# Another merged order for the steps of two batches in a two-layer decoder

## The chip, the cores and the metric

The kernel runs on one core of a Trainium2 chip. The metric is the device time of one launch in microseconds (us): the median of three launches. A profiled launch gives the trace from which all rows below are read; its span goes from the first to the last instruction. The engines are TensorE (PE, matrix products), VectorE (DVE), ScalarE (ACT, functions from tables), GpSimd (POOL) and SyncE (SP, which only issues DMA transfers).

## The reference

Six blocks follow each other on an input of 2 batches × 512 tokens × 128 features, each as `x = layernorm(x + f(x))`:

```
x = _layernorm(x + _L0_attn_ref(x, ...))    # Hawk: rmsnorm, conv of 4, gates, linear recurrence, gated MLP
x = _layernorm(x + _L0_xattn_ref(x, ...))   # cross attention, 8 heads, 32 context rows
x = _layernorm(x + _L0_ffn_ref(x, ...))     # causal attention, 16 heads of 8, RoPE; then 7 experts, top 2, + shared
x = _layernorm(x + _L1_attn_ref(x, ...))    # selective SSM, 16 states:
...
        h = a_t * h + bx_t
        y = jnp.einsum('bdn,bn->bd', h, c_t)
...
x = _layernorm(x + _L1_xattn_ref(x, ...))   # masked cross attention, FiLM, S4D convolution, FFN
x = _layernorm(x + _L1_ffn_ref(x, ...))     # 8 experts, top 2, and 2 shared ones:
...
        eo = jnp.einsum('eti,eih->eth', jax.nn.silu(hg) * hu, wd)
        y = jnp.einsum('te,eth->th', wdense, eo)
        shared = jax.nn.silu(xf @ swg) * (xf @ swu) @ swd
```

## The kernel before, in words

x stays on the chip transposed: features on the 128 partitions, 512 tokens along the free dimension (often in two halves of 256). There are three lanes of work. Lane a is batch 0 and lane b is batch 1; each goes through the six blocks. Lane w holds what depends on weights alone: the masks and constants of the gates, the tables of the S4D convolution (cosines, sines, powers, differences and their spectra), and the context tables.

Each compute engine's program is written as three generators, one for each lane. Every `next` of a generator issues one step (mostly one to eight instructions) and its waits; a step ends with an increment of a semaphore that belongs to its engine and lane. There are 541 steps on PE, 575 on DVE, 465 on ACT and 97 on POOL. The table `TURNS` gives for each engine the order in which the three lanes take their turns: `"a8 w1 a5"` is eight steps of batch 0, one shared step, five steps of batch 0. Inside a lane the order is fixed. `TURNS` is the only thing that decides which instruction stands behind which on an engine, and as an engine runs its instructions in order, a step that waits holds back all that is behind it, of the other lanes too. Waits name a step and not a place, so any merged order computes the same. A wait in a step is for a semaphore's count of another engine and lane (`pe.wait_ge(*after("act", b, f"su{n - 2}"))`).

`TABLES` belongs to ACT. Its functions come from four table sets (`exp`, `log`, `gelu`, `sin`); Exp is in `exp` and in `log`. `"232:exp"` loads the set for exp before step 232. A table load is an instruction of its own (L1203).

SP has one list of transfers in a fixed order, each behind the step that it waits for. It is not in `TURNS`.

Names that the text uses, by stage:

- Hawk: `h1` (first rmsnorm: square, log, exponents `ra`, `r`), z and g (projections), x1 (first residual), h2, X1 (the layernormed output). Helper lines are ACT L1207, DVE L1553 (tensor_tensor), L1556, L1559, L1562 (reduce), POOL L2195.
- Self attention: k1, k2, q1, q2 (RoPE products) give kk and qq, of which `kr, qr, kl, ql` take off high and middle parts, so that each is three bf16 pieces. SP writes the pieces to DRAM (L572, `draft_k`, `draft_q`) and reads them back stacked over partitions (L579). For batch 0 DVE does the splitting, for batch 1 POOL. On the stacked operands PE computes `mx` units (L821, L824: scores whose maximum DVE takes, eight pairs of heads × A to E) and then `su` units (L838, L841: 40 scores per batch, of which ACT takes the exponent), `pv` (L852, values), nmt1 (L859, the maxima turned over), yT and yt (transposes), mo (output projection).
- First experts: `sl` and `hu`, `hw` with L924, L929, L956; `rt` is the router; ln3 and X3 the layernorm behind them.
- SSM: dl, dx, `sc0` to `sc15` (DVE scans, L1878), `hc` (products with C), `by` (POOL products); X4 is the output.
- Shared S4D work: `s1..` on ACT, `r`, `q` and `P`, `Q`, `tP`, `tQ`, `aP`, `aQ` (DVE L1556 and L1559 on 1024 columns, POOL L2281); `z`, `a`, `dc` are small tables of 128 × 128.
- Second cross attention `xb`, FFN, and the second experts: 14 units of 128 per batch, with three pairs of 512-column products each (L924, L929, L956).

Every stage of batch 1 runs somewhat behind that of batch 0, and the order of the turns is what interleaves them.

Of the kernel before, what the change touches and what calls it, by code (L numbers as in the profile page):

```python
# [162 lines left out]
def _centre(t):  # L163
# [59 lines left out]

TURNS = {
# [8 lines left out]
    "dve":  # L233
# [8 lines left out]
    "act":  # L242
# [6 lines left out]
    "pool":  # L249
        "w13 b3 w1 b2 w1 b1 w37 a1 w1 a4 w1 a7 w1 a4 b1 a1 w1 b16 w1",  # L250
}

TABLES = (
# [4 lines left out]


def steps_of(engine, lane):
# [2271 lines left out]
```

## Time and profile before

| | |
|---|---|
| time, median of 3 (lowest, highest) | 487.06 us (486.44, 488.05) |
| span of the profiled execution | 484.9 us |
| median less the span | 2.2 us |
| mean granted TensorE clock | 0.927 |
| busy PE | 413.4 us, 85% |
| busy DVE | 333.5 us, 69% |
| busy ACT | 293.4 us, 61% |
| busy POOL | 125.2 us, 26% |
| table loads in the chain: ACT L1203 | 3% of the span |

The profiled execution gives no time besides its span; what lies around the span is taken as the 2.2 us between it and the median. Of the chain of work that ended last, PE has 58%, DVE 19%, ACT 12%. A busy share is a mean over stages with different limits; the stages are told apart by windows of 20 us. In a row of the timeline the first number is the start, the second the duration (of several merged instructions with `xN`), and the brackets at the end hold the idle time before it on its engine and what ended it.

### The profile page before, as it was taken

What the parts mean: (1) busy time and instruction counts of PE and PEld (TensorE: products, weight loads), DVE (VectorE), ACT (ScalarE), POOL (GpSimd) and SP (SyncE); (2) the same over time, 40 slices, a digit from 0 to 9 for tenths busy, and PEclk for the clock granted to TensorE, in tenths of its full rate; (3) what the DMA queues carried; (4) which work ended last, traced back from release to release, by engine and by line L of the source; (5) the groups of instructions that cost most, each with busy time, mean ns of one, the idle gap of its engine ahead of it and who ended that gap; (6) DMA issues with size and microseconds to landing.
All of it is one profiled execution on the core that took longest, in us unless ns stands there. A gap on an engine that the chain in (4) does not pass through costs nothing.

```text
span 484.9 us, 5925 instructions
## 1 busy us (share of the span) xinstructions
PE 413.4 (85%) x2035; PEld 202.0 (42%) x2035; DVE 333.5 (69%) x616; ACT 293.4 (61%) x508; POOL 125.2 (26%) x129
## 2 busy tenths in 40 slices
PE   5968988888889999999977875557889899999995
PEld 2443533443345554434343221232666544544442
DVE  1386567789969953562799999899977543564454
ACT  4865697526245678889576896456347575652125
POOL 1100000000382029007966667745000200000000
PEclk9999999958789999999997996667989999999999
DMA  8950000564181000005008857979500000501401
GB/s 280 341 153 30 1 2 0 170 90 150 50 191 25 2 4 3 2 15 161 0 18 239 211 168 214 213 206 278 230 0 1 1 0 17 159 1 53 123 0 43
DMA packets 26109, 46.62 MB, mean 96 GB/s; under 512 B 7397, under 2 KB 12742, under 8 KB 24918
## 3 DMA queue, kind: packets, MB, share of 16 engines
q1 hardware_dynamic: 25972, 46.15, 33.6%
q8 instruction: 16, 0.26, 0.3%
q10 hardware_dynamic: 108, 0.10, 0.1%
q14 instruction: 13, 0.11, 0.1%
HBM read 41.13 MB, written 5.01 MB: 95 GB/s over the span
## 4 chain that ended last, share of the span: by engine, by line
PE 58%; DVE 19%; ACT 12%; issue 5%; POOL 3%; DMA 2%; SPq 1%; DVEq 0%; ACTq 0%
ACT AR L1207 7%; DVE AR L1553 7%; PE PS L924 7%; PE PS L956 6%; PE PS L929 5%; PE PS L852 4%; PE PS L838 4%; PE PS L821 3%; ACT L1203 3%; PE PS L688 3%; PE PS L1007 2%; DVE stats L1562 2%; DVE AR L1559 2%; POOL AR L2195 2%; DVE AR L1878 2%
## 5 line engine op out<-in xcount | busy, mean ns | idle before, releaser
L1207 ACT ACTIVATE AR<-PS 128x512 f32<-128x512 f32 (+3 forms) x187 | 98.9, 563 | 103.3 <-PE PS L924 49.5
L1553 DVE TENSOR_TENSOR AR<-PS,AR 128x512 f32<-128x512 f32 (+1 forms) x104 | 69.1, 675 | 49.6 <-PE PS L929 30.4
L2195 POOL TENSOR_TENSOR AR<-AR 128x512 f32<-128x512 f32 (+2 forms) x48 | 52.5, 1101 | 137.3 <-DVE AR L1553 106.7
L1207 ACT ACTIVATE AR<-AR 128x256 f32<-128x256 f32 (+3 forms) x110 | 46.7, 463 | 44.3 <-DVE AR L1553 28.0
L1203 ACT ACT_TABLE_LOAD x42 | 53.9, 1283 | 0.8
L1562 DVE TENSOR_REDUCE stats<-PS 128x1 f32<-128x512 f32 (+4 forms) x88 | 43.6, 521 | 10.3 <-PE PS L762 4.3
L1878 DVE TENSOR_TENSOR_SCAN AR<-PS,AR 128x512 f32<-128x512 f32 x32 | 38.8, 1212 | 1.3 <-ACT PS L1207 0.7
L821 PE MATMUL PS<-RR 97*128 97x512 bf16 (+3 forms) x128 | 34.1, 344 | 4.2 <-DVE stats L1562 3.3
L688 PE MATMUL PS<-AR,W_sq 128*128 128x256 f32 x88 | 27.3, 424 | 10.8 <-ACT AR L1207 6.3
L1553 DVE TENSOR_TENSOR AR<-AR 128x512 f32<-128x512 f32 (+2 forms) x48 | 32.3, 689 | 3.9 <-ACT AR L1207 2.6
L1207 ACT ACTIVATE AR<-PS,W_vec 128x256 f32<-128x256 f32 (+1 forms) x46 | 24.2, 545 | 12.6 <-PE PS L688 4.3
L838 PE MATMUL PS<-RR 100*128 100x512 bf16 (+3 forms) x128 | 29.5, 302 | 2.5 <-ACT AR L1207 2.3
L2281 POOL TENSOR_TENSOR RR<-KL,lags 128x512 f32<-128x512 f32 x24 | 29.4, 1262 | 1.2 <-PE PS L841 1.1
L929 PE MATMUL PS<-x_in,RR 128*128 128x512 f32 x56 | 28.6, 596 | 0.0
L956 PE MATMUL PS<-AR,RR 128*128 128x512 f32 x56 | 28.5, 596 | 0.0
L1207 ACT ACTIVATE PS<-AR,RA 128x512 f32<-128x512 f32 x32 | 21.5, 684 | 11.5 <-DVE AR L1878 7.7
L924 PE MATMUL PS<-x_in,RR 128*128 128x512 f32 x56 | 28.4, 595 | 0.0
L688 PEld LDWEIGHTS PS<-AR,W_sq 128*128 128x128 f32 x88 | 15.9, 201 | 24.9 <-ACT AR L1207 16.2
L824 PE MATMUL PS<-W_bf 128*128 128x256 bf16 (+1 forms) x80 | 22.5, 282 | 0.0
L852 PE MATMUL PS<-AR,Vaug 128*9 128x512 f32 (+3 forms) x256 | 21.8, 434 | 0.0
L841 PE MATMUL PS<-W_bf 128*128 128x256 bf16 (+1 forms) x80 | 20.2, 252 | 0.0
L1710 DVE TENSOR_REDUCE stats<-PS 128x1 f32<-128x384 f32 x32 | 17.5, 548 | 3.5 <-PE PS L824 3.3
(241 smaller groups left out, 712.8 us busy)
## 6 DMA issues: line engine op xcount, KB each, us to landing
AR<-scan SPq DMA_DIRECT2D x64, 256.0 KB, 3.9
RR<-in_ffn SPq DMA_DIRECT2D x1, 2688.0 KB, 11.1
RR<-in_ones SPq DMA_DIRECT2D x2, 832.0 KB
RR<-in_ones SPq DMA_DIRECT2D x2, 784.0 KB
RA<-in_moe SPq DMA_DIRECT2D x1, 1539.5 KB, 6.2
AR<-weights SPq DMA_DIRECT2D x6, 256.0 KB, 4.8
W_mla<-in_mla SPq DMA_DIRECT2D x1, 1504.0 KB, 15.9
W_late<-in_late SPq DMA_DIRECT2D x1, 1076.0 KB, 11.5
```

The costliest lines, as they stand in the source:

```text
L688: mm(own(b, i)[:, c], w("sq", "ones"), A(b, 1)[:, c], start=True, stop=True)\
L821: mm(ring[:, c:c + n_], Qst[b][0:MROWS, h, 128 * qt:128 * qt + 128], Kst[b][0:MROWS, h, 0:n_], start=(qt, c) == segs[0][1:], stop=False)
L838: mm(ring[:, c:c + n_], Kst[b][0:KROWS, h, 128 * kb:128 * kb + 128], Qst[b][0:KROWS, h, 128 * kb:T], start=(c == 0), stop=False)
L924: mm(own(b, 0), w(group, "g", 128 * k, 128), x, start=True, stop=True)\
L929: mm(own(b, 1), w(group, "u", 128 * k, 128), x, start=True, stop=True)\
L956: mm(own(b, 3), w(group, "d", 128 * j, 128), A(b, 6 + j % 2), start=(j == 0 and base is None), stop=(k == n))\
L1203: nc.scalar.preload_act_table_set(tables[loaded[0]])
L1207: nc.scalar.activation(out_, in_, func, bias=bias, scale=scale).then_inc(*done("act", *step))
L1553: nc.vector.tensor_tensor(out_, a, b_, op).then_inc(*done("dve", *step))
L1562: nc.vector.tensor_reduce(out_, a, X, op).then_inc(*done("dve", *step))
L1878: nc.vector.tensor_tensor_scan(A(b, 14 + i % 2), own(b, 1 + 2 * (i % 2)), scan_row(b, "dx", i), 0.0, ALU.mult, ALU.add).then_inc(*done("dv ...
L2195: nc.gpsimd.tensor_tensor(out_, a, b_, op).then_inc(*done("pool", *step))
```

## The change

Only `TURNS` (all four engines) and `TABLES` are different. Steps, their waits, tiles, buffers and SP's list of transfers are as they were. Since the tables got shorter by three lines, every line of the file after it has a number smaller by three.

```
 TURNS = {
     "pe":
-        "a8 w1 a5 w2 a2 w1 a3 w1 a4 w2 a2 b2 a1 b2 a2 b1 a2 b1 a2 b2 a2 b2 ...
+        "a9 w1 a4 w3 a6 w1 a3 w2 a2 b2 a2 b2 a3 b2 a2 b1 a2 b3 a2 b1 a1 b1 ...
...
 TABLES = (
-    "2:log 11:gelu 12:log 14:gelu 17:exp 26:log 40:gelu 47:log 51:gelu 52:exp 64:log 91:gelu 100:log "
-    "125:sin 133:log 230:sin 232:exp 239:sin 245:exp 247:sin 254:log 272:sin 280:exp 282:sin 283:exp "
...
+    "2:log 11:gelu 14:exp 26:log 40:gelu 47:log 51:gelu 53:exp 65:log 92:gelu 96:sin 101:log 105:sin 107:log "
+    "230:sin 233:exp 240:sin 245:exp 248:sin 252:log 255:sin 257:log 273:sin 280:exp 282:sin 283:exp 285:sin "
...
```

The list has 42 table switches before and 45 after.

ACT, the first microseconds of the program (AR0 and x_in0 are batch 0, AR1 and x_in1 batch 1, `small` holds shared constants, `AR0<-AR0 128x256` are the exponents ra and r of h1). Before:

```order
2 L1207 ACTIVATE AR0<-x_in0 128x256 x2
3 L1203 ACT_TABLE_LOAD
4 L1207 ACTIVATE AR0<-PS 128x256 x2
5 L1207 ACTIVATE AR1<-x_in1 128x256
6 L1207 ACTIVATE AR0<-AR0 128x256 x2
7 L1207 ACTIVATE small<-W_vec 128x2
8 L1207 ACTIVATE AR0<-PS,W_vec 128x512 x2
9 L1207 ACTIVATE small<-small 128x2
10 L1203 ACT_TABLE_LOAD
11 L1207 ACTIVATE AR0<-PS 128x512
12 L1203 ACT_TABLE_LOAD
```

After:

```order
4 L1204 ACTIVATE AR0<-PS 128x256
5 L1204 ACTIVATE small<-W_vec 128x2
6 L1204 ACTIVATE AR0<-PS 128x256
7 L1204 ACTIVATE small<-small 128x2
8 L1204 ACTIVATE AR0<-AR0 128x256
9 L1204 ACTIVATE small<-small,W_vec 128x2
10 L1204 ACTIVATE AR0<-AR0 128x256
11 L1204 ACTIVATE AR0<-PS,W_vec 128x512 x2
12 L1200 ACT_TABLE_LOAD
13 L1204 ACTIVATE AR0<-PS 128x512 x2
14 L1204 ACTIVATE AR1<-x_in1 128x256
```

The square of batch 1's input moved from before the exponents of batch 0 to behind the first gelu of batch 0; three tiny shared exponents moved in between, and one pair of table switches is gone.

DVE around the splitting of batch 0 (`AR0<-AR0 128x512` are kk, qq, kr, qr, kl, ql in this order; `x_in1<-PS,AR1` is X1 of batch 1; `AR1<-AR1 128x128` are shared tables). Before:

```order
79 L1553 TENSOR_TENSOR AR0<-AR0 128x512 x2
80 L1553 TENSOR_TENSOR AR1<-PS,AR1 128x512
81 L1553 TENSOR_TENSOR AR0<-AR0 128x512
82 L1553 TENSOR_TENSOR AR1<-PS,AR1 128x512
83 L1553 TENSOR_TENSOR AR1<-AR1 128x128
84 L1553 TENSOR_TENSOR AR0<-AR0 128x512
85 L1553 TENSOR_TENSOR AR1<-AR1 128x128 x2
86 L1553 TENSOR_TENSOR AR0<-AR0 128x512 x2
87 L1553 TENSOR_TENSOR x_in1<-PS,AR1 128x256 x2
88 L1562 TENSOR_REDUCE stats<-PS 128x16
```

After:

```order
80 L1550 TENSOR_TENSOR AR0<-AR0 128x512 x2
81 L1550 TENSOR_TENSOR AR1<-PS,AR1 128x512 x2
82 L1550 TENSOR_TENSOR AR0<-AR0 128x512 x2
83 L1550 TENSOR_TENSOR x_in1<-PS,AR1 128x256 x2
84 L1550 TENSOR_TENSOR AR0<-AR0 128x512 x2
85 L1559 TENSOR_REDUCE stats<-PS 128x16
```

kl and ql of batch 0 stood ahead of batch 1's X1 and now stand behind it. The small shared tables are gone from here.

PE where the maxima of batch 0 end (L821/L824 with 512, 384+128, 256 columns are the mx units, L838/L841 the su units, L859 is nmt1, L852 pv0.0). Before:

```order
175 L824 MATMUL PS<-W_bf 128x2x128
176 L838 MATMUL PS<-RR 128x512
177 L841 MATMUL PS<-W_bf 128x128
178 L838 MATMUL PS<-RR 128x512
179 L841 MATMUL PS<-W_bf 128x128
180 L838 MATMUL PS<-RR 128x512
181 L841 MATMUL PS<-W_bf 128x128
182 L838 MATMUL PS<-RR 128x512
183 L841 MATMUL PS<-W_bf 128x128
184 L859 MATMUL PS<-W_bf,parts 24x128 x4
```

After:

```order
171 L821 MATMUL PS<-W_bf 128x2x128
172 L835 MATMUL PS<-RR 128x512
173 L838 MATMUL PS<-W_bf 128x128
174 L835 MATMUL PS<-RR 128x512
175 L838 MATMUL PS<-W_bf 128x128
176 L818 MATMUL PS<-RR 128x512
177 L821 MATMUL PS<-W_bf 128x128
178 L835 MATMUL PS<-RR 128x512
179 L838 MATMUL PS<-W_bf 128x128
180 L818 MATMUL PS<-RR 128x384
181 L818 MATMUL PS<-RR 128x128
182 L821 MATMUL PS<-W_bf 128x256
```

Row 176 of after is the first maxima unit of batch 1. Before, it stood behind su5, nmt1 and pv0.0 of batch 0; now it stands behind su1, and the units of the two batches alternate from there.

Other moves that the text speaks of: on ACT, b.rt went from behind a.ln3's exponents to before its logs; on DVE, batch 0's X4 went from behind b.sc3 to behind b.hc4; on POOL, the shared dc1 to dc12 went from behind b.kr to before b.kk, and aP1 and aQ1 went from before a.dx to behind a.by1 and a.by5.

## Rows read from the trace of the kernel before

**Rows 1.** Windows of 20 us, PE: length, busy (instructions), granted clock, DMA share, GB/s.
```profile
180.00:200.00 20.00, 19.74 (x176) 1.00 0.01 3
...
440.00:460.00 20.00, 20.00 (x52) 1.00 0.39 107
```
**Rows 2.** The same windows, DVE.
```profile
100.00:120.00 20.00, 18.60 (x42) 0.76 0.44 118
320.00:340.00 20.00, 19.76 (x25) 0.78 0.89 231
```
**Rows 3.** Timeline, ACT, the exponents of h1 of batch 0.
```profile
8.68 0.42 ACT L1207 ACTIVATE AR<-x_in 128x256 f32<-128x256 f32 x1 [1.76 <-DMA x_in<-in_x]
9.00 0.70 ACT L1207 ACTIVATE AR<-AR 128x256 f32<-128x256 f32 x2
```
**Rows 4.** Timeline, PE, first projection of batch 0.
```profile
9.76 0.82 PE L696 MATMUL PS<-W_sq 128*128 128x512 bf16 x3 [0.70 <-ACT AR L1207]
11.33 1.10 PE L716 MATMUL PS<-AR,RA 128*128 128x512 f32 x2 [0.75 <-DVE AR L1559]
```
**Rows 5.** Timeline, DVE, x1 of batch 0.
```profile
40.34 0.69 DVE L1553 TENSOR_TENSOR AR<-PS,x_in 128x512 f32<-128x512 f32 x1 [1.26 <-PE PS L735]
```
**Rows 6.** Timeline, DVE, RoPE and splitting of batch 0, X1 of batch 1.
```profile
84.66 1.29 DVE L1553 TENSOR_TENSOR AR<-PS,W_mla 128x512 f32<-128x512 f32 x2 [0.93 <-PE PS L792]
...
90.39 2.61 DVE L1553 TENSOR_TENSOR AR<-AR 128x128 f32<-128x128 f32 x6
94.97 0.76 DVE L1553 TENSOR_TENSOR x_in<-PS,AR 128x256 f32<-128x256 f32 x2 [1.97 <-ACT AR L1207]
```
**Rows 7.** Timeline, PE and DVE, the first maxima unit of batch 0.
```profile
100.10 0.61 PE L821 MATMUL PS<-RR 97*128 97x512 bf16 x1 [0.53 <-ACT Vaug L1207]
...
103.43 0.63 DVE L1562 TENSOR_REDUCE stats<-PS 128x1 f32<-128x512 f32 x1
```
**Rows 8.** Timeline, POOL and SP: dc1 after kr of batch 1; last stack transfer of its first heads.
```profile
132.22 0.46 POOL L2195 TENSOR_TENSOR KL<-AR,KL 128x128 f32<-128x128 f32 x1 [1.43 <-ACT AR L1207]
...
138.34 0.42 SPq L579 DMA_DIRECT2D RR<-draft_q  x1
```
**Rows 9.** DMA of 136 to 139 us: issues, KB each, us to landing.
```profile
RR<-draft_k SPq DMA_DIRECT2D x1, 192.0 KB, 4.0
```
**Rows 10.** Timeline, PE, between the maxima of the two batches.
```profile
140.92 0.39 PE L838 MATMUL PS<-RR 100*128 100x512 bf16 x1 [0.41 <-ACT AR L1207]
...
142.68 0.39 PE L859 MATMUL PS<-W_bf,parts 128*24 128x128 bf16 x4 [0.82 <-DVE parts L1553]
...
144.75 0.39 PE L821 MATMUL PS<-RR 97*128 97x512 bf16 x1
```
**Rows 11.** Timeline, PE, the longest wait in the overlap of the two attentions.
```profile
201.75 0.39 PE L838 MATMUL PS<-RR 100*128 100x256 bf16 x2 [0.89 <-ACT AR L1207]
```
**Rows 12.** Timeline, POOL, shared products beside batch 0's third layernorm.
```profile
233.20 15.86 POOL L2281 TENSOR_TENSOR RR<-KL,lags 128x512 f32<-128x512 f32 x12
```
**Rows 13.** Timeline, ACT, the router of batch 1.
```profile
245.82 0.23 ACT L1207 ACTIVATE stats<-stats 128x28 f32<-128x28 f32 x1 [0.48 <-DVE stats L1553]
```
**Rows 14.** Timeline, DVE, up to the first scan.
```profile
243.62 2.07 DVE L1559 SCALAR_TENSOR_TENSOR RR<-RR 128x1024 f32<-128x1024 f32 x1
...
249.20 1.21 DVE L1559 SCALAR_TENSOR_TENSOR RR<-RR 128x1024 f32<-128x1024 f32 x1
...
252.47 0.68 DVE L1553 TENSOR_TENSOR AR<-AR 128x512 f32<-128x512 f32 x1
...
262.33 1.21 DVE L1878 TENSOR_TENSOR_SCAN AR<-PS,AR 128x512 f32<-128x512 f32 x1
```
**Rows 15.** Timeline, ACT, a table switch in the scans.
```profile
280.11 1.28 ACT L1203 ACT_TABLE_LOAD   x1
281.40 0.60 ACT L1207 ACTIVATE AR<-PS 128x512 f32<-128x512 f32 x1
```
**Rows 16.** Timeline, DVE, X4 of batch 0 among the scans of batch 1.
```profile
315.24 0.76 DVE L1553 TENSOR_TENSOR x_in<-PS,AR 128x256 f32<-128x256 f32 x2 [1.72 <-ACT AR L1207]
```

More of the change, by code:

```diff
@@ L225 @@
     "pe":
[7 rows of a table removed]
-    "dve":
[8 rows of a table removed]
-    "act":
[6 rows of a table removed]
[6 rows of a table added]
+    "dve":
[7 rows of a table added]
+    "act":
[5 rows of a table added]
     "pool":
-        "w13 b3 w1 b2 w1 b1 w37 a1 w1 a4 w1 a7 w1 a4 b1 a1 w1 b16 w1",
+        "w25 b4 w1 b1 w2 b1 w22 a3 w1 a4 w1 a1 w1 a2 w1 a2 w1 a4 b1 a1 w1 b16 w1",
 }
 TABLES = (
[4 rows of a table removed]
[4 rows of a table added]
 def steps_of(engine, lane):
```

43 rows, old and new, of tables (TABLES, TURNS) are left out of this document.

## The prediction
> **What bounds the kernel now.** I read the windows of 20 us first. Between about 143 and 206 us PE has no gaps to speak of (19.74 of 20 us busy in one window of it [rows 1]), and in the second experts, from about 400 us, it is busy all the time (20.00 of 20 at 440 to 460 us [rows 1]). In both the same multiplications must be done whatever the order, so there an order can win or lose only what PE waits. In between DVE is the bound: it has 18.60 of 20 us at 100 to 120 us, where it takes batch 0's maxima, and 19.76 at 320 to 340 us in the scans [rows 2]. What is left is chains in which no engine is full: the first 100 us, the first experts of batch 0 (206 to 262 us), the second cross attention (345 to 400 us) and the end behind the last product. Then I read the timelines of the stretches in which the two orders differ, and followed each lane's chain through them. A change of order moves no work off the chip, so its effect is the sum of the waits that it takes from these chains and puts into them. All times of the trace are of the profiled execution, with a span of 484.9 us; the median of the runs is 2.2 us above it, and I add that at the end.
>
> **Step 1, the start: −2.6 us.** ACT waits 1.76 us for batch 1's input and squares it (0.42 us), and only then gives batch 0's exponents at 9.00 us [rows 3]. PE waits for them 0.70 us at 9.76 us, and for DVE's product 0.75 us at 11.33 us [rows 4]. After, three exponents of two columns stand there and the square is behind the first gelu. The exponents can start when ACT is done at 6.92 us (8.68 less 1.76), so up to 2.1 us earlier; the filler products of PE (0.82 us in that row, and those ahead) still stand before the projection, so I take 1.7 us for it. One pair of table switches goes from the same chain (2 × 1.28 us [rows 15]), of which I count 0.9, since ACT waits for PE in that stretch anyway. x1 of batch 0, at 40.34 us before [rows 5], comes 2.6 us earlier. Bounds: −1.0 (only what PE waits after the exponents) and −4.7 (2.1 and both switches).
>
> **Step 2, up to batch 0's maxima: +0 to the sum, but all late things are later.** The small shared tables that DVE did one by one beside kr to ql (six steps in 2.61 us at 90.39, four of them tables [rows 6]) now go earlier, into DVE's waits. In exchange k1 of batch 0 stands before batch 1's input product, so that this waits for what k1 waits for (0.93 us before 84.66 [rows 6]), and batch 1's X1 stands ahead of kl and ql. It waits 1.97 us for ACT at 94.97 [rows 6] and comes over 1 us later for the reason just given. So kl and ql, which ended at 93.00 us (90.39 + 2.61), end at about 98.2, measured in the time of before (that is, with step 1 left out; so are all times up to step 7). The write to DRAM and the stacking behind them move by 5.2 us. PE had its first maxima product at 100.10 us [rows 7], and DVE took it only at 103.43 us [rows 7], since it was still in batch 1's cross attention; this slack of 3.3 us is the cover. The first stack lands at about 103.7 by my count, 3.6 us after 100.10, so the cover is used up and the start of the maxima is about 1 us late. DVE gets that back: it is rid of the small tables that stood between the maxima. The last maximum of batch 0 comes at +0.3 us. Bounds 0 and +2.
>
> **Step 3, the middle: +1.9 us.** This is the step that I believe most. Batch 1's pieces are split on POOL. dc1 waited 1.43 us there at 132.22 us behind kr [rows 8]; dc1 to dc12 now stand before kk, and kk itself comes 1.3 us later, because batch 1 has become later in step 2. I get ql at +1.7 us, and so the last transfer for the first heads at 140.0 instead of 138.34 us [rows 8]. A neighbour of 192 KB took 4.0 us from issue to landing [rows 9]; with 3.6 the stack is there at 143.6 us. On PE batch 1's first maxima unit was at 144.75 us [rows 10], behind su2 to su5, nmt1 and pv0.0 of batch 0, so that it never waited. Now it stands behind su1 alone. PE reaches it at about 140.9 us, where su2 stood [rows 10], waits until 143.6, and has the other units still to do: they take 144.75 − 140.92 − 0.82 (the wait of nmt1) = 3.0 us [rows 10]. So it is at the same point at 146.6 instead of 144.75. From there to 206 us PE is full, and nothing gives it back. Bounds: −0.8 (the stack is there in time, and the wait of 0.82 goes) and +3.3 (the stack lands 1.4 us later than I count, which batch 0's own transfers ahead of it in the queue could do).
>
> **Step 4, the overlap of the attentions: +0.9 us.** The end of batch 0's attention moves ahead by 8 to 16 places among batch 1's score units, and with it ten short steps of ACT squeeze in between its exponents. Before, the longest such wait of PE was 0.89 us at 201.75 [rows 11], and the sum over 180 to 200 us 0.26 us (20 less 19.74 [rows 1]), 1.2 us in all. For after I count 2.1 us. That batch 0 ends sooner brings nothing, since its first sl on ACT stands behind b.su33 in both. Bounds 0 and +1.6.
>
> **Step 5, first experts of batch 0 up to the scans: −0.1 us.** Batch 1's router exponent, which waited for DVE at 245.82 us [rows 13], now stands before the logs of batch 0's ln3. This and POOL's products at the same time make X3 late by some 2.9 us. But X3 was not what DVE waited for: the SSM's dl ran at 252.47 [rows 14] behind a chain of small router operations, and then the shared q at 261 us ran until the scan at 262.33 [rows 14]. POOL's 12 products of 15.86 us [rows 12] lie over this stretch and stretch DVE's operation from 1.21 to 2.07 us (249.20 and 243.62 [rows 14]). Of these twelve, aP1 and aQ1 now go behind by1 and by5, and dl gets +0.9 but the rest −1.0. Bounds −1 and +2.9 (X3's delay in full). On this stretch the Trainium skill ("SBUF — State Buffer", the shared port pair) has a rule that an operation of VectorE with two inputs in SBUF and one of GpSimd fully block each other; the 0.86 us by which the one row is longer than the other agrees in sign, and by the rule aP1 and aQ1 would only move the price into the scans' stretch, where DVE's products with one input in PSUM don't pay it.
>
> **Step 6, the scans: −0.4 us.** DVE is full here, so only its idle time counts. Two more table switches on ACT and a shared sine moved forward cost +0.6 at the tenth scan, and batch 1's products of POOL begin behind the shared Q1: +0.8 at its first scan. Batch 0's X4 waited 1.72 us for ACT at 315.24 [rows 16]; it stands two scans' places later now, with work of batch 1 ahead of it, and this wait goes, of which 0.5 comes back at the next one. −1.2. Bounds −1.7 and +2.5 (a scan waits for both of the switches). A table switch shows here as 1.28 us and the next function starts 0.01 us after it [rows 15]. The Trainium skill ("ScalarE: Activation LUTs", *What ACT_TABLE_LOAD costs*) gives 1283 ns for the load and some 1380 ns for a drain, 2.66 us in all, by which three more switches would take 8.0 us of ACT and not 3.9; the row shows no such drain.
>
> **Step 7, 345 us to the end: +0.1 us.** PE's order is the same in nearly all of this. Units 10 to 13 of batch 0 are drawn ahead and batch 1's come alone at the end; with 20.00 of 20 us busy [rows 1] that is the same sum of products. Bounds 0 and +0.6.
>
> **Sum.** −2.6 + 0 + 1.9 + 0.9 − 0.1 − 0.4 + 0.1 = −0.2 us. The span would be 484.7 us, the time 486.9 us. The change is many small gains and losses of opposite sign, and the early gain is eaten before 145 us. What a measurement tells from no change here is 0.3%, 1.5 us.
>
> **Rivals.** *A, the early gain survives: about 484.2 us.* If the stack lands at about 142 us, since the queue is shorter than I think, step 3 is at 0, and with half of step 4 the sum is −2.6 + 0 + 0.5 − 0.1 − 0.4 + 0.1 = −2.5, and 484.6; with the whole 1.72 us of rows 16 gained 484.2. For it: PE waited 0.82 us for nmt1 in that very place [rows 10], and the new order offers it work there; the landing in step 3 rests on a chain of four delays that I worked out. Against it: kl and ql behind X1, which the order shows plainly.
> *B, PE's queue stalls behind late stacks: about 490 us.* One mechanism, at two places: the operands of the maxima. If kl and ql end 1 us later than 98.2, batch 0's maxima start that much later and DVE, at 18.60 of 20 us [rows 2], has nothing to catch up with; the same at batch 1's unit gives +3.3 in place of +1.9, and a further 1.3 us where the other heads' transfers come later than the exponents of batch 0. −2.6 + 1 + 3.3 + 1.3 + 0.9 − 0.1 − 0.4 + 0.1 = +3.5, and 490.6. It decides from the point where the first stack lands after 104.7. For it: SP's list is in fixed order, so one late piece delays all behind it. Against: the slack of 3.3 us at 103.43.
> *C, batch 0's chain after its attention is what matters: about 489 us.* X3 is late by 2.9 us and DVE is not covered by the router, so the scans start 2 us later: +1.9.
>
> **Chances.** My forecast and what lies within 0.3% of before: 0.37. A, and other ways to over 1.5 us faster: 0.34. B 0.18, C 0.08, others slower 0.03, so slower in all 0.29. The case A is so near in chance because the only sure gain is at the start and all that eats it is counted. The range goes from 483.8 (A) to 490.2 (nearly B); the forecast's own range is 485.6 to 488.5.
>
> **What would show it.** Step 1: x1 of batch 0 near 37.7 us. Step 2: kl, ql of batch 0 end near 95.6 on the new clock (98.2 − 2.6), and the first maximum of DVE near 101.9. Step 3: a wait of PE of about 2.5 us before batch 1's first maxima unit, and that unit near 141 us. Step 4: waits of some 2 us in all from 176 to 206 us. Step 5: first scan near 262.4. Step 6: no wait for ACT at X4, last scan of batch 1 within 0.5 us of before. The forecast is wrong if PE doesn't wait at batch 1's first unit, or if the first scan is over 1.5 us away from 262.3.

## The result, and the profile after

The changed kernel took 494.38 us (median of 4 runs, 491.55 to 500.76) against 487.56 us for the kernel before (4 runs, 486.44 to 488.23). The ratio is 1.0126, with a 95% interval from 1.0089 to 1.0163: 6 to 7 us slower. A second set gave 495.22 us (6 runs, 492.60 to 500.47) against 486.79 us, ratio 1.017 (1.012 to 1.022). I had forecast 486.9 us, no change. Medians are over all runs of a kernel; the ratios leave out runs that are over 1.5% above its fastest one.

The first profiled execution of the changed kernel was the slowest of its runs (span 498.9 us). The rows below are from its second trace (span 494.3 us, mean granted clock 0.927, the same as before), where not said otherwise. The first trace is late from the start (+1.6 us at x1, +4.8 at batch 0's last maxima unit) and ends at +14.1. All line numbers of the changed kernel are smaller by three. The columns are as ahead of the prediction. "Lag" is the time at which a step ends, less the time of the same step in the trace of before.

The start. ACT gives the exponents at 6.89 us and not at 9.00 [rows 3], as forecast; PE's projection begins at 10.23 us (11.33 before [rows 4]); but the projection in front of x1 takes 3.61 us, and x1 of batch 0 is at 40.37 us, where it was before (40.34 [rows 5]). ACT, PE, DVE:

```profile
6.89 0.41 ACT L1204 ACTIVATE AR<-AR 128x256 f32<-128x256 f32 x1
```
```profile
10.23 3.60 PE L713 MATMUL PS<-AR,RA 128*128 128x512 f32 x8
...
36.73 3.61 PE L732 MATMUL PS<-AR,RA 128*128 128x512 f32 x4
```
```profile
40.37 0.69 DVE L1550 TENSOR_TENSOR AR<-PS,x_in 128x512 f32<-128x512 f32 x1 [2.62 <-PE PS L732]
```

The same four products in front of x1 in the trace of before, PE:

```profile
38.05 2.25 PE L735 MATMUL PS<-AR,RA 128*128 128x512 f32 x4
```

Batch 0's kl and ql end at 97.28 us (96.00 + 1.28; 93.00 before [rows 6]) and PE waits 3.95 us for their stack; DVE takes the first maximum at 103.75 us (103.43 before [rows 7]). DVE, then PE, then DVE:

```profile
95.33 0.76 DVE L1550 TENSOR_TENSOR x_in<-PS,AR 128x256 f32<-128x256 f32 x2 [3.76 <-ACT AR L1204]
96.00 1.28 DVE L1550 TENSOR_TENSOR AR<-AR 128x512 bf16<-128x512 f32 x2
```
```profile
102.59 0.58 PE L818 MATMUL PS<-RR 97*128 97x512 bf16 x1 [3.95 <-DMA RR<-draft_q]
```
```profile
103.75 0.68 DVE L1559 TENSOR_REDUCE stats<-PS 128x1 f32<-128x512 f32 x1
```

Batch 1's first maxima unit, which never waited before [rows 10], now waits 2.47 us for its last stack transfer, at 142.40 us. The product of 512 columns takes 0.38 us ahead of the wait, 0.63 us behind it and 0.38 us again later (148.22; the products of 146.14 us are already fast): behind the wait PE ran at half its clock. PE:

```profile
139.50 0.38 PE L835 MATMUL PS<-RR 100*128 100x512 bf16 x1
...
142.40 0.44 PE L818 MATMUL PS<-RR 97*128 97x512 bf16 x1 [2.47 <-DMA RR<-draft_q]
142.74 0.63 PE L835 MATMUL PS<-RR 100*128 100x512 bf16 x1
...
148.22 0.38 PE L818 MATMUL PS<-RR 97*128 97x512 bf16 x1
```

This wait is not in the first trace of after. There PE is at half clock from 130 to 150 us, gets to the unit later and waits 0.65 us, for ACT:

```profile
144.73 0.63 PE L835 MATMUL PS<-RR 100*128 100x512 bf16 x1
...
146.12 0.61 PE L818 MATMUL PS<-RR 97*128 97x512 bf16 x1 [0.65 <-ACT Vaug L1204]
```

The windows of the second trace, PE: granted clock (the number behind the bracket) 0.83 and 0.85, where in before both are 1.00 ([rows 1] for the one from 180 us):

```profile
140.00:150.00 10.00, 7.58 (x49) 0.83 0.83 119
180.00:190.00 10.00, 7.95 (x67) 0.85 0.01 3
```

But the window from 140 us is at 0.83 also in four of the six traces whose order is that of before from 20 to 205 us, and these four have spans of 484.2 to 492.4 us. One of them is the run that only moved a square at the start (485.62 us, below); there PE comes out of a wait of 0.94 us at nmt1 at half clock. PE, window, then timeline:

```profile
140.00:150.00 10.00, 9.15 (x72) 0.83 0.63 93
```
```profile
140.85 0.47 PE L859 MATMUL PS<-W_bf,parts 128*24 128x128 bf16 x4 [0.94 <-DVE parts L1553]
141.25 0.61 PE L838 MATMUL PS<-RR 100*128 100x384 bf16 x2
```

The end of batch 1's maxima: four operations of DVE on 32 columns (nh1, nr1, nm1, nl1) take 1.09, 0.99, 0.96 and 0.98 us, while POOL begins its twelve shared products at 181.42 us, and PE waits for them. DVE, POOL, PE:

```profile
181.43 1.09 DVE L1553 TENSOR_SCALAR parts<-stats 128x32 bf16<-128x32 f32 x1
182.55 0.99 DVE L1556 SCALAR_TENSOR_TENSOR stats<-stats,parts 128x32 f32<-128x32 f32 x1
183.57 0.96 DVE L1565 CAST parts<-stats 128x32 bf16<-128x32 f32 x1
184.56 0.98 DVE L1550 TENSOR_TENSOR parts<-stats,parts 128x32 bf16<-128x32 f32 x1
```
```profile
181.42 13.56 POOL L2278 TENSOR_TENSOR RR<-KL,lags 128x512 f32<-128x512 f32 x12 [27.68 <-PE PS L838]
```
```profile
185.60 0.39 PE L856 MATMUL PS<-W_bf,parts 128*24 128x128 bf16 x4 [1.83 <-DVE parts L1550]
...
187.60 1.11 PE L901 MATMUL PS<-W_sq,AR 128*128 128x128 f32 x4 [0.21 <-DVE AR L1550]
188.64 1.88 PE L849 MATMUL PS<-AR,Vaug 128*9 128x512 f32 x8
```

In the trace of before the first of these four was at 176.70 us and POOL's products began at 180.49 us. DVE, POOL:

```profile
176.70 0.18 DVE L1556 TENSOR_SCALAR parts<-stats 128x32 bf16<-128x32 f32 x1
176.92 0.19 DVE L1559 SCALAR_TENSOR_TENSOR stats<-stats,parts 128x32 f32<-128x32 f32 x1
```
```profile
180.49 13.59 POOL L2281 TENSOR_TENSOR RR<-KL,lags 128x512 f32<-128x512 f32 x12 [1.11 <-PE PS L841]
```

The scans of both batches now wait for POOL, where in before the first of all followed directly upon another operation [rows 14]; X4 still waits 1.22 us for ACT (1.72 before [rows 16]). DVE:

```profile
270.83 1.22 DVE L1875 TENSOR_TENSOR_SCAN AR<-PS,AR 128x512 f32<-128x512 f32 x1 [3.60 <-POOL AR L2192]
...
316.37 1.22 DVE L1875 TENSOR_TENSOR_SCAN AR<-PS,AR 128x512 f32<-128x512 f32 x1 [2.41 <-POOL AR L2192]
...
327.47 0.75 DVE L1550 TENSOR_TENSOR x_in<-PS,AR 128x256 f32<-128x256 f32 x2 [1.22 <-ACT AR L1204]
```

The lag through the trace (us), and that of three mixtures that are explained below:

| step | after | after, block back | before to 205, then after | after to su33, then before |
|---|---|---|---|---|
| x1 of a | 0.0 | −0.7 | −1.0 | −1.0 |
| last maxima unit of a (PE) | −0.6 | −1.5 | −2.1 | −1.9 |
| nmt1 of b | +6.9 | +3.6 | −2.3 | +4.9 |
| su33 of b (ACT) | +7.0 | +2.4 | −2.1 | +5.3 |
| first scan of a | +8.5 | +3.6 | 0.0 | +5.4 |
| first scan of b | +10.3 | +4.8 | +0.5 | +3.9 |
| X6 of b | +9.5 | +5.3 | +0.3 | +5.2 |

### The profile page after: what moved, and what is told of

Its sections match the earlier page's. It is cut to its first block, busy times and chain, and to the rows that moved or that the text cites. A ratio compares the mean times of both kernels' runs of the same rounds, so it can differ in the third digit from the quotient of the medians.

```text
span 498.9 us, 5926 instructions
## 1 busy us (share of the span) xinstructions
PE 422.9 (85%) x2033; PEld 202.5 (41%) x2035; DVE 336.3 (67%) x616; ACT 297.7 (60%) x511; POOL 124.9 (25%) x129
## 4 chain that ended last, share of the span: by engine, by line
PE 62%; DVE 15%; ACT 13%; issue 4%; POOL 4%; DMA 2%; SPq 0%; DVEq 0%; ACTq 0%
ACT AR L1204 8%; PE PS L953 6%; PE PS L921 6%; PE PS L926 6%; DVE AR L1550 5%; PE PS L818 4%; PE PS L835 3%; PE PS L685 3%; PE PS L722 3%; PE PS L849 3%; POOL RR L2278 3%; DVE AR L1875 2%; ACT L1200 2%; PE PS L1004 2%; PE PS L693 2%
## 5 line engine op out<-in xcount | busy, mean ns | idle before, releaser
L1204 ACT ACTIVATE AR<-PS 128x512 f32<-128x512 f32 (+2 forms) x187 | 98.6, 561 | 106.1 <-PE PS L921 44.9
L818 PE MATMUL PS<-RR 97*128 97x512 bf16 (+3 forms) x128 | 35.1, 352 | 7.1 <-DVE stats L1559 3.8
L2278 POOL TENSOR_TENSOR RR<-KL,lags 128x512 f32<-128x512 f32 x24 | 27.7, 1186 | 27.8 <-PE PS L838 27.7
L835 PE MATMUL PS<-RR 100*128 100x512 bf16 (+3 forms) x128 | 30.5, 311 | 2.0 <-ACT AR L1204 1.9
L821 PE MATMUL PS<-W_bf 128*128 128x256 bf16 (+1 forms) x80 | 23.2, 289 | 0.0
L818 PEld LDWEIGHTS PS<-RR 97*128 97x128 bf16 x128 | 11.4, 107 | 25.5 <-DVE stats L1559 14.6
L987 PE MATMUL PS<-AR,RA 128*32 128x512 f32 x64 | 12.6, 871 | 10.3 <-DVE AR L1550 10.3
```

The costliest lines, as they stand in the source:

```text
L818: mm(ring[:, c:c + n_], Qst[b][0:MROWS, h, 128 * qt:128 * qt + 128], Kst[b][0:MROWS, h, 0:n_], start=(qt, c) == segs[0][1:], stop=False)
L835: mm(ring[:, c:c + n_], Kst[b][0:KROWS, h, 128 * kb:128 * kb + 128], Qst[b][0:KROWS, h, 128 * kb:T], start=(c == 0), stop=False)
L1204: nc.scalar.activation(out_, in_, func, bias=bias, scale=scale).then_inc(*done("act", *step))
```

## The experiments

"Mixture" means: the steps up to a place stand in one kernel's order, all others in the other's; steps, waits and buffers are the same in all kernels here, and the table switches follow the order of ACT. Each ratio is to runs of the kernel before on the same chip, with its 95% interval; the runs were made on three chips, so runs of different chips are best compared by their ratios.

**The changed kernel again.** No edit.

> The changed kernel unchanged, to have a second trace of it. Its four runs so far lie between 491.6 and 500.8 us, and the one trace (span 498.9) is the slowest of them. If the loss lies in places (theory P), this trace shows the same waits in a shorter span: PE waits 1.5 to 2 us at batch 1's nmt1, and nh1, nr1, nm1, nl1 take about 1.0 us each on DVE (before 0.19). If the loss is only a lower granted clock of that one run (theory C), this trace has neither and ends within 2 us of before.

495.22 us, ratio 1.017 (1.012 to 1.022). The waits of the first trace are there again in a trace of the same mean clock as before (nmt1 1.83 us, the four small operations about 1.0 us each). For these theory P holds: the loss lies in places. The wait at batch 1's first maxima unit is not one of them: 2.47 us here, 0.65 us in the first trace.

**POOL's products away from the four small operations.**

```
 PE, from batch 1's su0 (a and b are the batches):
-b.su0 a.su38 a.su39 b.su1 b.su2 a.pv3.1 a.pv3.2 b.su3 b.nmt1 a.yT3
+b.su0 a.su38 b.su1 b.su2 b.su3 b.nmt1 a.su39 a.pv3.1 a.pv3.2 a.yT3
```

> The changed kernel, with su39 (and pv3.1, pv3.2 behind it) of batch 0 moved on PE behind nmt1 of batch 1. The last score unit of batch 0 releases POOL's twelve products of the S4D tables. Theory P: these products stretch the four small DVE operations of batch 1's maxima from 0.19 to 1.0 us each, PE waits 1.84 us for them, and its clock falls to half for the 4 us behind: with the move the four are back at 0.2 us, PE does not wait, and the kernel gains 2.5 to 4 us. Theory C or a loss that lies elsewhere: within 0.5 us of the changed kernel.

497.45 us, ratio 1.0169 (1.0114 to 1.0224): no gain in the time. The mechanism is shown all the same: su39 of batch 0 releases POOL, and with it behind, the four take 0.18 to 0.19 us. DVE:

```profile
185.42 0.18 DVE L1555 TENSOR_SCALAR parts<-stats 128x32 bf16<-128x32 f32 x1
185.64 0.19 DVE L1558 SCALAR_TENSOR_TENSOR stats<-stats,parts 128x32 f32<-128x32 f32 x1
185.86 0.18 DVE L1567 CAST parts<-stats 128x32 bf16<-128x32 f32 x1
```

The wait of 1.83 us at nmt1 is gone, and three others come in its place, of PE:

```profile
186.27 0.39 PE L837 MATMUL PS<-RR 100*128 100x512 bf16 x1 [0.53 <-ACT AR L1206]
...
189.61 0.66 PE L867 MATMUL PS<-W_sq,AR 128*128 128x128 f32 x4 [0.72 <-ACT AR L1206]
...
191.79 0.66 PE L903 MATMUL PS<-W_sq,AR 128*128 128x128 f32 x4 [0.86 <-DVE AR L1552]
```

Against the first trace of after, whose start was alike (lag 8.6 and 8.4 us at batch 1's last maxima unit), the lag at su33 is 1.4 us less. I had expected 2.5 to 4.

**Two mixtures around 145 us.**

> All steps that started before 145 us in the trace of before stand in the order of before, the others in the order of after. If the loss is made behind 145 us (theory P: nmt1, then the first experts), this has it nearly whole: 490 to 492 us, 3 to 5 us over before. If it is made ahead of 145 us (theory E: the late pieces of batch 0 and the clock of PE), this is within 1.5 us of before.

495.76 us, ratio 1.0187 (1.0149 to 1.0225). Nearly the whole loss, but not a clean part: its trace has a wait of 3.95 us of DVE for POOL's memset at 148.00 us, which neither kernel has; the seam made it.

> The reverse: all steps that started before 149 us in the trace of after stand in the order of after, the others in the order of before. Theory P: within 1.5 us of before, or a little faster; theory E: 4 us or more slower than before. If both halves cost, each of the two mixtures is slower than before by a part and the parts add up to that of the changed kernel.

491.50 us, ratio 1.0101 (1.0066 to 1.0136). In these six runs the early part costs 4.7 us by itself, against theory P. In its trace the lag is −0.8 us at x1, +2.0 at batch 0's last maxima unit and +3.6 at batch 1's, so over half of it was lost ahead of 142 us (the expectation of the run with the block back, below, says that all was lost between 139 and 159 us; that is wrong). And PE does not wait for the stack at batch 1's first unit. It is at half clock from 128 to 148 us and waits 0.65 us for ACT. PE, timeline, then window:

```profile
143.35 0.61 PE L822 MATMUL PS<-RR 97*128 97x512 bf16 x1 [0.65 <-ACT Vaug L1208]
```
```profile
140.00:150.00 10.00, 9.35 (x48) 0.58 0.84 129
```

**The start alone.**

```
 ACT:
-a.h1.l b.h1.sqa a.h1.ra a.h1.r ... w.fb.l b.h1.sq
+a.h1.l a.h1.ra a.h1.r ... w.fb.l b.h1.sqa b.h1.sq
```

> The kernel before, with one step moved on ACT: the square of batch 1's first half of the input goes from before batch 0's exponents of the first rmsnorm to just before its own second half. My theory of the start (step 1): x1 of batch 0 comes earlier, by 1.2 us (what PE's first projection gained in the traces of after) as long as PE's clock stays high; 1 to 2 us faster in all. Rival (clock): the emptier PE falls to the low clock in the first 40 us (projection rg 3.6 in place of 2.25 us), and the time is within 0.5 us of before or above it.

485.62 us, ratio 1.0018 (0.9984 to 1.0052): no gain. PE's first projection is 2.0 us earlier in this trace, x1 1.1 us; but seven other traces with the old start have x1 at −1.5 to +0.5, so 1 us of start is within what one execution differs from the next. My forecast took it from a single trace.

**Batch 1's first units early, alone.**

```
 PE (with v of batch 1 on ACT ahead of su1):
-a.su0 a.su1 a.su2 a.su3 a.nmt1 a.su4 a.su5 a.pv0.0 b.mx0.A b.mx0.B b.mx0.C
+a.su0 a.su1 b.mx0.A a.su2 b.mx0.B a.su3 b.mx0.C a.nmt1 a.su4 a.su5 a.pv0.0
```

> The kernel before, with the first three maxima units of batch 1 on PE drawn ahead to behind su1, su2 and su3 of batch 0, as in the changed kernel (and v of batch 1 on ACT ahead of su1, which they need). Theory (step 3): PE waits at the first unit for the last stack transfer, issued at 138.34 us; with 3.6 us to land that is until 142 us, a wait of about 1 us, in place of the wait of 0.8 at nmt1 that moves behind it: 0 to +1 us at the same point, since here the stack is not late. Rival (clock): any wait of PE between 140 and 145 us keeps the clock at half for the following 5 us, 2 to 3 us slower.

485.68 us, ratio 1.0018 (0.9983 to 1.0053): no loss. PE waits, but 1.31 us and not 2.47, and the products behind stay at 0.38 us. PE:

```profile
139.41 0.38 PE L822 MATMUL PS<-RR 97*128 97x512 bf16 x1 [1.31 <-DMA RR<-draft_q]
139.69 0.38 PE L839 MATMUL PS<-RR 100*128 100x512 bf16 x1
```

**The block back behind pv0.0, with the early order of after.**

> All steps up to batch 0's last maxima unit on PE (139 us) in the order of after, the others in the order of before, so that batch 1's first unit stands behind pv0.0 again. The mixture that changed over at 149 us was 4.7 us slower than before, and its trace lost all of this between 139 and 159 us. Theory (step 3: the unit's place makes the loss): this one is 2 to 4 us faster than that mixture, 488 to 489.5. Rival (the late stack and the low clock at 130 to 150 us make it, wherever the unit stands): 491 us again.

485.81 us, ratio 0.9985 (0.9944 to 1.0026). Its 12 runs fall into two groups, 481.7 to 485.8 (7) and 489.4 to 493.9 (5). The ratio counts the lower group alone; the mean of all twelve is 487.6 us, against 485.8 for the kernel before.

The mixture at 149 us differs from this one by the place of the block (and of v of batch 1 on ACT). Its median is 5.7 us higher, but that is not shown to be the price of the place. Its six runs (489.9 to 494.0, on another chip) lie where the upper group of this one lies. The two traces, both of runs in that range, need 68.3 us (149) and 67.8 us (this one) from batch 0's last maxima unit to batch 1's su33, only 0.6 us apart, both at half clock for most of 128 to 150 us. This one's window, PE:

```profile
140.00:150.00 10.00, 9.84 (x45) 0.51 0.97 170
```

Whether the early block makes the upper group come more often (6 of 6 runs against 5 of 12) is not settled. That late kl and ql of batch 0 cost nothing by themselves is shown by the two runs at the end of this section.

**The same in the changed kernel, and both mends.** mx0.A to mx0.D of batch 1 behind pv0.0 of batch 0; then also su39 as above.

> The changed kernel, with the first four maxima units of batch 1 on PE put back behind pv0.0 of batch 0, as in the kernel before. The order up to 139 us alone cost nothing (485.8), the order up to 149 us cost 4.7 us, and what lies between the two is this block. Theory (the place of the block, met by a late stack): 3 to 5 us faster than the changed kernel, 490 to 492. Rival (the block alone is harmless, as it was in the kernel before, and the loss comes from the two orders of PE behind 145 us): less than 1.5 us faster.

490.78 us, ratio 1.0084 (1.0053 to 1.0116), against 1.017 (1.012 to 1.022) for the second set of the changed kernel: by these, 4 us of the 8 are this block. Against its first set (1.0126, 1.0089 to 1.0163) it is 2 us, and the intervals overlap. In the traces the stretch from batch 0's last maxima unit to batch 1's su33 takes 71.3 us, against 75.1 and 74.0 in the two traces of the changed kernel.

> The same, and su39, pv3.1 and pv3.2 of batch 0 behind nmt1 of batch 1, so that POOL's twelve products no longer stand beside the four small DVE operations. Theory: 1.2 to 3 us faster than with the first mend alone (that is what the trace of that mend gained), 488 to 490. Rival: the waits only move to the next places, as at su3, yT3 and yt in the trace of the single mend, and the gain is under 0.5 us.

492.54 us, ratio 1.0125 (1.0082 to 1.0169). The second mend gains nothing on top of the first; the rival was right, as the same three waits of 0.53, 0.72 and 0.86 us take the place of one that was only 0.88 us here.

**Behind 205 us.**

> All steps that started before 205.5 us in the trace of before in the order of before, the others in the order of after. In the second trace of after the lag was 7.0 us at the end of batch 1's scores and 9.5 at the end, with 8.5 at the first scan and 10.1 at the last. Theory: the order behind 205 us costs by itself 2 to 3.5 us (POOL's shared products in the scans delay by0 of batch 1, X3 late): 489 to 490.5. Rival (what follows is only the lag carried on, with PE's clock): within 1 us of before.

488.48 us, ratio 1.0087 (1.0051 to 1.0124). The order behind 205 us costs 2 to 4 us by itself. Both waits for POOL are there (its lag rises from −2.1 at su33 to 0.0 at the first scan), DVE:

```profile
262.29 1.22 DVE L1877 TENSOR_TENSOR_SCAN AR<-PS,AR 128x512 f32<-128x512 f32 x1 [3.49 <-POOL AR L2194]
...
306.61 1.22 DVE L1877 TENSOR_TENSOR_SCAN AR<-PS,AR 128x512 f32<-128x512 f32 x1 [2.40 <-POOL AR L2194]
```

> The order of after up to batch 1's su33 (214 us in its trace), then the order of before. The reverse mixture was 2 to 4 us slower than before. Theory (the two parts add up): this is 3 to 5 us faster than the changed kernel, 490 to 492, so still 4 us slower than before. Rival (behind 205 us the lag is only carried on): as slow as the changed kernel.

490.30 us, ratio 1.0081 (1.0046 to 1.0117): the parts add up, 0.8% and 0.9% to the 1.7% of the whole. Its lag stays at 5.2 to 5.3 us from su33 to the end, but for the scans, where it falls for a while.

> The order of before up to 205 us, then that of after, but POOL in the order of before throughout (aP1 and aQ1 ahead of dx of batch 0, U11, U21, V1 and Q1 in their old places). The mixture with after's POOL order was 4.2 us slower than before by the ratio of the fast runs, and its DVE waited 2.40 us for POOL at batch 1's first scan, against 0.56. Theory: POOL's order is 1 to 2 us of it. Rival: with the old order DVE's r and q operations are stretched again (1.2 to 2.07 us each) and X3 stays late, so nothing is gained.

493.25 us, ratio 1.0136 (1.0098 to 1.0174), against 1.0087 (1.0051 to 1.0124) with after's POOL order. DVE still waits 2.42 us at batch 1's first scan. So POOL's new order is not what costs here, and my theory of this run was wrong.

> The order of before up to 205 us and then that of after, with batch 1's router exponent on ACT back behind batch 0's ln3 exponents. The mixture without this was 4.2 us slower than before by the ratio, its ACT waited in front of this step, and X3 was ready 2.2 us later against its surroundings. Theory: it gains 1.3 to 2 us over that mixture, and dl and the first scan come 1.3 to 2 us earlier. Rival (dl is held by other work of DVE): under 0.5 us.

487.68 us, ratio 1.0064 (1.0036 to 1.0092). The first scan is at +0.9 with a lag of +0.7 at su33, so 1.9 us better than in the mixture without it (−2.1 to 0.0). The times differ by 0.8 us (on two chips), and the intervals overlap; part of the loss is likely there, not shown to be.

> The kernel before, with that one step alone moved on ACT: batch 1's router exponent ahead of batch 0's ln3 logs. Theory: ACT waits for DVE's lg there (245.8 us), ln3 is about 1.7 us later, X3 too, and the first scan about 1 us; 0.5 to 1.5 us slower. Rival (the r and q operations of DVE hold the first scan): within 0.3 us of before.

486.27 us, ratio 1.0002 (0.9980 to 1.0023): this step alone does nothing in the kernel before.

**PE's own start, and the best of both.** kv of the shared lane ahead of z3 again on PE; then also kl and ql of batch 0 ahead of batch 1's X1 on DVE.

> The mixture that has the order of after up to 139 us and then that of before, with PE's first 27 steps (up to batch 0's rg) in the order of before: kv stands ahead of z3 again, so that PE waits for DVE ahead of its gates only once it has done both. That mixture had 7 runs of 481.7 to 485.8 and 5 of 489.4 to 493.9 us. Theory (PE's clock falls at 17 us when PE runs dry earlier, and all 5 slow ones are that): with the old start of PE no run is over 489, median about 484. Rival (ACT's and DVE's early order makes PE's activity uneven, whatever its own order): both groups are there again.

485.27 us, ratio 0.9990 (0.9959 to 1.0020). The mean of all 12 runs is 485.6 us, that of before 485.8. 2 of the 12 are over 489 us (489.7, 490.2), where it was 5 of 12 without, on another chip.

> The same, and kl and ql of batch 0 on DVE ahead of batch 1's X1 as in the kernel before, so that the first stack is not late (ql ended 4.3 to 6.7 us later in the traces of after). Theory: the maxima of batch 0 start 1 to 2.5 us earlier: 1 us faster than the mixture without this, and 1 to 2 us faster than the kernel before. Rival: DVE is full in the maxima anyway and nothing is gained: within 0.5 us of the mixture.

485.31 us, ratio 0.9999 (0.9970 to 1.0028). Early kl and ql gain nothing, and nothing beats the kernel before. That fits the rival (DVE is full in the maxima), which no run tells from other causes.

## Why the prediction was wrong, by its steps

On the lag of the second trace the steps come to: x1 0.0 (forecast −2.6), from there to batch 0's last maxima unit −0.6 (0), to batch 1's su33 +7.6 (steps 3 and 4, +2.8), to the last scan of batch 1 +3.1 (steps 5 and 6, −0.5), to the end −0.7 (+0.1). Together that is +9.4 us and not −0.2. The largest error is in steps 3 and 4.

**Step 1 (−2.6 us): the rows were right, the gain isn't there.** The exponents came 2.1 us earlier, the projection only 1.1, as PE's filler products stood ahead of it for longer. The other 1.5 us that I counted I had taken from gaps of one execution; x1 varies by 2 us between executions of one start order. Over the traces of the old start (seven, without the run that moved the square) x1 is at −0.6 on average, over the five traces of the new start without the fall of the clock told of below at −0.6 as well. The head start that was to pay for the rest did not exist.

**Step 2 (0): about right.** The stack of batch 0 was late (PE waits 3.95 us) and DVE took it back: the first maximum was at 103.75 against 101.9 forecast, the last unit of batch 0 on PE at −0.6. (Of the six steps of DVE at 90.39 us three were tables and not four, which changes nothing in the sum.)

**Step 3 (+1.9): the step that failed, in its size, and right in its wait by luck.** The wait was forecast at about 2.5 us and measured as 2.47, but not for the reason given. The last transfer for batch 1's first heads was to be issued 1.7 us late, and it went out at 138.20 us, where it was before (138.34 [rows 8]). PE came at 139.93 (forecast, without step 1, 140.9), and the stack took 4.2 us from issue to PE's start and not 3.6. In the first trace this wait was 0.65 us, for ACT. As the wait of 0.82 us at nmt1 and one of 0.41 us were gone [rows 10], the waits up to 150 us grew by only 1.2 us.

What I left out is what PE does behind its waits: its products ran at half clock from 142.6 to 146 us and again from 187 to 190 us. Between batch 0's last maxima unit and batch 1's su33 the trace of after needs 8.3 us more (75.06 against 66.77) in nearly the same steps. 3.7 us are more waits (6.29 against 2.58), 2.9 us are steps that last longer at 140 to 150 and 185 to 190 us, 0.9 us are two products of the first experts that now stand ahead of su33, and 0.8 us stay open. So in this trace the clock cost nearly as much as the waits. Its first half, at 142.6 us, can't be put down to the change, since four of six traces with the old order have it too; with that alone, the run with the moved square needs 1.5 us more for this stretch (68.25) at the same waits (2.56). The second half goes with the wait of step 4: all four traces with a wait of 1.83 us at batch 1's nmt1 have a stretch of half clock behind it, and none of the other fourteen has one between 160 and 220 us. The block's place was worth 2 to 4 us of the 6 to 8, by the run that puts it back.

**Step 4 (+0.9): too small, as an interaction was missed.** I followed POOL's twelve products only as something that delays q and r of DVE. But their releaser is su39 of batch 0, which the new order lets run before the end of batch 1's maxima. In after the four small operations and the products collide, for 3.3 us of DVE (4.0 in place of 0.7), a wait of 1.83 us and half clock behind it. PE's waits from 176 us to su33 come to 3.5 us and not to the 2.1 that I counted. The rows to see this were there: the release of POOL by PE's score unit at 180.49 us, 3 us behind nl1, and the same price on a short operation beside two products of POOL (from 255.37 us) in the trace of before, DVE:

```profile
256.51 0.97 DVE L1568 CAST parts<-stats 128x28 bf16<-128x28 f32 x1
```

The rule of the Trainium skill that I weighed at step 5 ("SBUF — State Buffer", the shared port pair: an operation of VectorE or GpSimd that needs the pair fully blocks while the other engine holds it) says just this. The trace agrees: 0.18 becomes about 1.0 us, nearly as long as one of POOL's products (13.56 us for 12). I had applied it to long operations, where it stretches by 0.9 us in 1.2; on a short one it is fivefold. Putting the four operations ahead of POOL's products took this wait away, but the time did not fall, as other waits took its place.

**Step 5 (−0.1) and 6 (−0.4): wrong in sign.** X3 was late as forecast (+3.3 against its surroundings, forecast +2.9), and dl by 1.4 (forecast 0.9). But the shared q in front of the first scan was no cause of its time in before, it filled a wait: the chain dl, dx, spread over DMA, scan needs 9.9 and 10.0 us (252.47 to 262.33; 260.84 to 270.83), and 9.6 to 10.3 us in fifteen of the sixteen other traces (10.7 in one). So a late dl was a late scan, and DVE stood 3.60 us. At X4 the wait did not go (1.22 of 1.72 us remain). Together the two steps cost 3.1 us in after (lag +7.0 at su33, +10.1 at the last scan of batch 1) and 3.8 in the mixture at 205 us, where the forecast had a gain of 0.5. (The terms given in step 6, +0.6, +0.8 and −1.2, make −0.4 only if the second holds the first.)

**Step 7 (+0.1): right.** From the last scan of batch 1 to the end the lag changes by −0.7 us.

Of the rivals, B (PE's queue stalls behind late stacks) named the place and was forecast at 490.6; that the sign was open I had put at 0.29 for slower. By its own words it decided from a stack later than 104.7 us, and that did not happen. The late stack of batch 0 was harmless, and that of batch 1 was not late: it was PE that came early. So B came nearest in its time and not by its mechanism.

**Not settled.** In three of eight traces with after's early order, PE's gate products at 17 us take 8.80 us and not 7.10 (first trace of after against the second, PE), and in none of ten with the old start of PE.

```profile
16.96 8.80 PE L722 MATMUL PS<-AR,RA 128*128 128x512 f32 x16 [0.92 <-DVE AR L1556]
```
```profile
16.48 7.10 PE L722 MATMUL PS<-AR,RA 128*128 128x512 f32 x16 [0.92 <-DVE AR L1556]
```

These traces have spans of 490.0 to 498.9 us. The runs over 489 us fell from 5 to 2 of 12 with PE's start put back, which points to it, but is too few to show it. The mixture at 149 us has all its runs over 489 us, and its trace has 7.11 us here, so this is not the only way to such a time. What in the order behind 205 us costs the rest, beyond the router's exponent, is open too, and so is what the rest of the order between 149 us and su33 costs: with the block back the changed kernel is still 4 us slower than before, of which the order behind 205 us makes 2 to 4.

## What to carry to other kernels

Where a merged order is changed, look for the waits that it makes in front of a full engine, and look at the clock behind each: here 3.7 us more of waits stood beside 2.9 us of slower products. Then look whether the same fall of the clock is also in traces of the old order; half of it was. A move that is harmless alone can cost among others (batch 1's early units: ratio 1.0018 alone, 2 to 4 us in the changed kernel), so try parts alone and together. Before counting on a gain of 1 to 2 us in the first stage, or explaining one trace, compare the same milestone in several executions.

## What was not expected of the hardware

DVE operations of 32 columns rise from 0.18 to 1.0 us beside POOL's products of 1.1 us, and stay at 0.18 where POOL starts only behind them (at 187.63 us, they at 185.42 to 186.27). Behind a wait of 1.31 us PE stayed at its high clock in one trace (products of 0.38 us on both sides), and behind one of 0.94 us in another its products took 0.61 us and more. So the length of the one wait did not decide it alone. And one order of instructions can have two groups of times (481.7 to 485.8 and 489.4 to 493.9 us).
